# ScalarE writes the high parts of keys and queries straight from PSUM, and VectorE's subtraction frees the bank

## What is computed

```python
x = x + xattn(layernorm(x), ctx, ctx, mask, W_q, W_k, W_v, W_o)   # x 32x100x128, ctx 32x1444x128
x = x + ffn(layernorm(x), gate_w, w1, w2)                          # 8 experts, best 2 per token

# xattn: 16 heads of 8
q = split(Q @ W_q.T); k = split(K @ W_k.T); v = split(V @ W_v.T)
scores = clip(einsum('bhqd,bhkd->bhqk', q, k) / sqrt(8), -50, 50)
attn = exp(scores) / sum(exp(scores))
out = einsum('bhqk,bhkd->bhqd', attn, v) @ W_o.T
```

## Time and profile before

| | |
|---|---|
| median of 3 runs | 1106.81 us (1106.25 to 1107.64) |
| the profiled execution's own time | 1106.66 us |
| its span, first to last instruction | 1104.9 us |
| granted TensorE clock, mean of the span | 0.969 |
| TensorE busy | 94% |
| ScalarE busy | 70% |
| VectorE busy | 69% |
| GpSimd busy | 22% |

### The profile page before, as it was taken

How to read it: one execution, slowest core, us unless ns; L and a number is a source line. 1 busy time by engine, 2 the same in 40 slices (tenths; PEclk the granted TensorE clock), 3 DMA queues, 4 the chain that set the end, 5 groups by cost and what they waited for, 6 DMA issues and landing times.

```text
span 1104.9 us, 32396 instructions
## 1 busy us (share of the span) xinstructions
PE 1033.4 (94%) x10544; PEld 759.8 (69%) x10545; DVE 761.0 (69%) x2088; ACT 769.6 (70%) x1088; POOL 240.0 (22%) x320
## 2 busy tenths in 40 slices
PE   5789999999999999999999999999999999399990
PEld 3567677777777677777677777777767776299990
DVE  4567777777777777777777777777777777444433
ACT  2567877777777877777877777877778777144430
POOL 3331111111111111111111111111111111245554
PEclk8899999999999999999999999999999999699995
DMA  7645555455555554555455555555555544022216
GB/s 217 186 154 166 173 170 170 165 166 167 168 171 170 172 171 164 173 167 170 167 171 173 173 173 173 174 174 174 174 174 174 174 157 142 23 68 63 65 49 178
DMA packets 144319, 172.71 MB, mean 156 GB/s; under 512 B 32235, under 2 KB 88559, under 8 KB 144287
## 3 DMA queue, kind: packets, MB, share of 16 engines
q1 hardware_dynamic: 138622, 165.26, 45.4%
q0 software_dynamic: 4896, 6.63, 2.2%
q10 hardware_dynamic: 768, 0.41, 0.2%
HBM read 36.83 MB, written 22.08 MB: 53 GB/s over the span
## 4 chain that ended last, share of the span: by engine, by line
PE 90%; DMA 3%; POOL 2%; SPq 2%; DVE 1%; issue 1%; ACT 1%; ACTq 0%; POOLq 0%; DVEq 0%
PE scores L753 31%; PE o_sum L765 26%; PE scratch L687 7%; PE scratch L676 7%; PE scores L873 5%; PE scores L884 5%; PE scratch L671 4%; PE scratch L726 1%; SPq L535 1%; POOL w_sb L597 1%; PE scratch L681 1%; PE scratch L731 1%; DMA x_all<-in_x_dram 1%; DMA q_stack<-q_rep 1%; PE scratch L747 1%
## 5 line engine op out<-in xcount | busy, mean ns | idle before, releaser
L990 ACT ACTIVATE probs<-scores 128x800 f32<-128x800 f32 (+1 forms) x640 | 615.2, 975 | 160.7 <-PE scores L753 158.6
L753 PE MATMUL scores<-q_stack,k_stack 128*128 128x400 f32 x1536 | 415.2, 380 | 10.5 <-DMA q_stack<-q_rep 8.1
L1136 DVE TENSOR_SCALAR probs<-probs 128x800 f32<-128x800 f32 (+1 forms) x640 | 396.2, 654 | 25.2 <-ACT probs L990 25.0
L753 PEld LDWEIGHTS scores<-q_stack,k_stack 128*128 128x128 f32 x1536 | 249.2, 190 | 110.5 <-issue 100.9
L765 PE MATMUL o_sum<-probs,v_both 128*17 128x200 f32 x6144 | 316.3, 335 | 0.1
L765 PEld LDWEIGHTS o_sum<-probs,v_both 128*17 128x17 f32 x6144 | 151.1, 97 | 132.4 <-issue 71.9
L630 POOL DMA_INDIRECT expert_rows<-rows,row_atu x64 | 75.6, 1181 | 408.8 <-DVE row_atu L1233 361.4
L687 PE MATMUL scratch<-w_turned,ctxT 128*128 128x128 f32 x768 | 102.5, 277 | 0.0
L687 PEld LDWEIGHTS scratch<-w_turned,ctxT 128*128 128x128 f32 x768 | 101.2, 194 | 0.0
L1073 DVE COPY v_both<-scratch 128x512 f32<-128x512 f32 x93 | 64.4, 692 | 42.4 <-PE scratch L687 42.4
L1048 DVE CAST k_hi<-k_full 128x512 fp32r<-128x512 f32 (+1 forms) x93 | 38.4, 412 | 79.5 <-ACT k_full L932 79.4
(11 more groups left out here) (145 smaller groups left out, 771.1 us busy)
## 6 DMA issues: line engine op xcount, KB each, us to landing
k_stack<-k_hi SPq DMA_DIRECT2D x192, 256.0 KB, 2.5
k_stack<-k_lo SPq DMA_DIRECT2D x192, 256.0 KB, 2.6
expert_rows<-fill SPq DMA_DIRECT2D x32, 406.2 KB
xT_and_ctx<-in_ctx_dram SPq DMA_DIRECT2D x16, 704.0 KB
ctx_nat<-in_ctx_dram SPq DMA_DIRECT2D x16, 704.0 KB
q_rep<-q_parts SPq DMA_DIRECT2D x124, 50.0 KB, 1.9
q_stack<-q_rep SPq DMA_DIRECT2D x124, 50.0 KB, 1.9
v_both<-expert_rows SPq DMA_DIRECT2D x57, 65.0 KB, 1.8
```

Source lines behind the costliest of these rows:

```text
L753: last = nc.tensor.matmul(score_banks(c)[:, m, :], k_stack[p][:, g, t * P:(t + 1) * P], q_stack[p][:, :, g, :], start=True, stop=True)
L990: nc.scalar.activation(probs_of(c), score_banks(c), ACT.Exp, scale=SCALE).then_inc(exp_ready, 1)
L1136: nc.vector.tensor_scalar(chunk, chunk, LOW, HIGH, ALU.max, ALU.min).then_inc(probs_ready, 1)
```

## The change

ScalarE's copy of a key or query step now goes straight into the high part, `k_hi` or `q_parts[:, 0]`, and takes over the wait for the DMAs that read that tile before. VectorE waits for ScalarE's copy and subtracts the high part from the bank in PSUM; this subtraction now frees the bank. The copies `k_full` and `q_full`, VectorE's casts of them, and the semaphore `q_split` are gone; SP, and ScalarE for the first queries, wait for the bank to be freed instead (`k_split` stays for the first batch). The expert stage, which used a part of `k_full`, has a tile of its own (`hidden_sb`). Order and chunks of the steps stay.

```diff
--- before.py
+++ after.py
@@ -198,8 +198,7 @@
                    sb("ctx_nat1", [P, TILES, D])[:]]
         w1_sb = xT_and_ctx[:, 0:E * F].rearrange("p (e f) -> p e f", e=E)
         ctxT = sb("ctxT", [P, TILES * P])
-        k_full = sb("k_full", [P, KSTEPS, KC * P])
-        q_full = sb("q_full", [P, SQ])
+        hidden_sb = sb("hidden_sb", [P, 2, FC * P])
         k_hi = sb("k_hi", [P, TILES * P], F32R)
         k_lo = sb("k_lo", [P, TILES * P], F32R)
         k_stack = [sb(f"k_stack{p}", [P, GROUPS, TILES * P], F32R) for p in range(2)]
@@ -271,7 +270,7 @@
         tile_home = [sb(f"tile_home{n}", [P, 1], U32) for n in range(NB)]
         w1_tile = ctxT[:, 0:2 * F].rearrange("p (n f) -> p n f", n=2)
         tileT = ctxT[:, 2 * F:2 * F + 2 * P].rearrange("p (n r) -> p n r", n=2)
-        hiddenT = k_full[:, 0:2, :].rearrange("p n (c r) -> p n c r", c=FC)
+        hiddenT = hidden_sb[:].rearrange("p n (c r) -> p n c r", c=FC)
 
         y_all = [probs[0:SQ].rearrange("p u q -> p (u q)")[:, 0:B * D].rearrange("q (b d) -> q b d", b=B),
                  xT_and_ctx[0:SQ, 0:E * F].rearrange("q (b d) -> q b d", b=B)]
@@ -318,7 +317,6 @@
         scratch_emptied = [sem(f"scratch_emptied{n}") for n in range(2)]
         k_hi_ready = sem("k_hi_ready")
         k_split = sem("k_split")
-        q_split = sem("q_split")
         k_stacked = [sem(f"k_stacked{k}") for k in range(KSTEPS)]
         scores_ready = sem("scores_ready")
         exp_ready = sem("exp_ready")
@@ -395,6 +393,16 @@
             first = FIRST_UNIT[c] % RING_UNITS
             return probs[:, first:first + UNITS[c], :]
 
+        def keys_split_at(b, k):
+
+            return scratch_use(b - 1, STEPS.index(("key", k)))
+
+        def queries_split_at(n):
+
+            if isinstance(n, int) and n < 2:
+                return divmod(ALONE.index(("first query", n)), 2)[::-1]
+            return scratch_use(n - 2, STEPS.index(("query", 0)))
+
         def all_emptied(engine, b, n):
 
             for late in range(2):
@@ -450,7 +458,12 @@
             def stack_keys(p, b):
 
                 for k in range(KSTEPS):
-                    sp.wait_ge(k_split, KSTEPS * b + k + 1)
+                    if later(b):
+                        bank, use = keys_split_at(b, k)
+                        sp.wait_ge(scratch_emptied[bank], use + 1)
+                        carry_wait(sp, sp_passed)
+                    else:
+                        sp.wait_ge(k_split, k + 1)
                     cols = slice(k * KC * P, (k + 1) * KC * P)
                     for t, part in enumerate((k_hi, k_lo, k_hi, k_lo)):
                         sp.dma_start(k_stack[p][t:P:4, :, cols].bitcast(F32),
@@ -458,7 +471,8 @@
 
             def spread_queries(n):
 
-                sp.wait_ge(q_split, n + 1)
+                bank, use = queries_split_at(n)
+                sp.wait_ge(scratch_emptied[bank], use + 1)
                 carry_wait(sp, sp_passed)
                 if later(n):
                     sp.wait_ge(q_stacked, QD * n)
@@ -927,16 +941,15 @@
                 elif name == "turn":
                     nc.scalar.copy(ctxT[:, KEY_COLS[k]], scratch[:, bank, 0:KEYS[k]]).then_inc(scratch_emptied[bank], 1)
                 elif name == "key":
-                    if later(b):
-                        act.wait_ge(k_split, KSTEPS * (b - 1) + k + 1)
-                    nc.scalar.copy(k_full[:, k, 0:KEYS[k]], scratch[:, bank, 0:KEYS[k]]).then_inc(scratch_emptied[bank], 1)
+                    act.wait_ge(k_stacked[k], KD * b)
+                    nc.scalar.copy(k_hi[:, KEY_COLS[k]], scratch[:, bank, 0:KEYS[k]]).then_inc(k_hi_ready, 1)
                 elif name == "first query":
                     if k:
-                        act.wait_ge(q_split, k)
-                    nc.scalar.copy(q_full[:], scratch[:, bank, 0:SQ]).then_inc(scratch_emptied[bank], 1)
+                        act.wait_ge(q_spread, QS * k)
+                    nc.scalar.copy(q_parts[:, 0, :], scratch[:, bank, 0:SQ]).then_inc(q_hi_ready, 1)
                 elif name == "query":
-                    act.wait_ge(q_split, b + 1)
-                    nc.scalar.copy(q_full[:], scratch[:, bank, 0:SQ]).then_inc(scratch_emptied[bank], 1)
+                    act.wait_ge(q_spread, QS * (b + 1))
+                    nc.scalar.copy(q_parts[:, 0, :], scratch[:, bank, 0:SQ]).then_inc(q_hi_ready, 1)
                 elif name == "queries":
                     nc.scalar.copy(attnT[:], scratch[:, bank, 0:SQ]).then_inc(scratch_emptied[bank], 1)
                 else:
@@ -954,7 +967,8 @@
 
             def spread_first():
 
-                act.wait_ge(q_split, 1)
+                bank, use = queries_split_at(0)
+                act.wait_ge(scratch_emptied[bank], use + 1)
                 for t in range(4):
                     act.dma_start(q_rep[t:P:4, :, :].bitcast(F32), q_parts[:, t // 2, :].bitcast(F32)).then_inc(q_spread, 16)
 
@@ -1042,24 +1056,16 @@
 
                 cols = KEY_COLS[k]
                 bank, use = at
-                dve.wait_ge(scratch_emptied[bank], use + 1)
-                if later(b):
-                    dve.wait_ge(k_stacked[k], KD * b)
-                nc.vector.tensor_copy(k_hi[:, cols], k_full[:, k, 0:KEYS[k]]).then_inc(k_hi_ready, 1)
                 dve.wait_ge(k_hi_ready, KSTEPS * b + k + 1)
-                nc.vector.tensor_tensor(k_lo[:, cols], k_full[:, k, 0:KEYS[k]], k_hi[:, cols].bitcast(F32),
-                                        ALU.subtract).then_inc(k_split, 1)
-
-            def split_queries(b, at):
+                nc.vector.tensor_tensor(k_lo[:, cols], scratch[:, bank, 0:KEYS[k]], k_hi[:, cols].bitcast(F32),
+                                        ALU.subtract).then_inc(scratch_emptied[bank], 1)
+
+            def split_queries(n, at):
 
                 bank, use = at
-                dve.wait_ge(scratch_emptied[bank], use + 1)
-                if later(b):
-                    dve.wait_ge(q_spread, QS * b)
-                nc.vector.tensor_copy(q_parts[:, 0, :], q_full[:]).then_inc(q_hi_ready, 1)
-                dve.wait_ge(q_hi_ready, b + 1)
-                nc.vector.tensor_tensor(q_parts[:, 1, :], q_full[:], q_parts[:, 0, :].bitcast(F32), ALU.subtract
-                                        ).then_inc(q_split, 1)
+                dve.wait_ge(q_hi_ready, n + 1)
+                nc.vector.tensor_tensor(q_parts[:, 1, :], scratch[:, bank, 0:SQ], q_parts[:, 0, :].bitcast(F32),
+                                        ALU.subtract).then_inc(scratch_emptied[bank], 1)
 
             def split(name, k, b, at):
```

## The result

The changed kernel takes 1121.86 us (median of 4 runs, 1120.6 to 1122.3) beside 1106.53 us of the kernel before on the same chip: ratio 1.0135, 95% interval 1.0118 to 1.0153. It is slower by 15.3 us; the forecast was 21.2 us slower, and 1121.9 lies 0.6 us under its range. The profiled execution took 1121.89 us, its span is 1120.0 us.

A forecast was written before the change was run, and what follows sets the result against it. TensorE was taken to pace the loop: 30 batches times a 0.72 us pause is 21.6, minus 0.4 for the first batch, plus 21.2 us on 1106.66, giving 1127.9 us; range 1122.5 to 1136.

The forecast's parts named there:

- The one cost: Query after key 1: the bank is freed later, by VectorE's subtraction, so TensorE stands 0.72 us in each batch.
- Rival 1: Loop: the ring of score banks, not TensorE, sets the pace and absorbs the pause; 1106.3 us; chance 0.06.
- Rival 2: Loop: each of 30 pauses lowers TensorE's clock, costing 1.7 us as after an earlier pause; 1179 us; chance 0.02.
- Casts in the loop: Loop: VectorE's key casts, 38.4 us in all, lie beside TensorE's work, so removing them is worth 0.
- The subtraction: VectorE's subtraction reading PSUM stays at 0.69 us for a full step, despite the skill's larger fixed cost.
- ScalarE's rounding copy: ScalarE's key copy into the rounded tile stays at 0.56 us mean; upper case 0.10 us more for a full step.
- The moved waits of ScalarE and SP: ScalarE's copies wait for earlier DMAs, SP for the subtraction under another semaphore; ScalarE's key-copy wait was judged free.
- the bound of 0.24: Very start: the first query's cast leaves, ScalarE's second query copy waits; between minus and plus 0.24 us, taken as 0.
- Nothing is spare: Query after key 1: its load came as the scores ran out, so the later bank costs 0.72 us, start against start.
- minus 0.4: First batch: a 2 us query pause is absorbed by TensorE's later GpSimd wait; GpSimd's chain starts 0.4 us earlier.

The follow-up runs named there:

- the doubled run: Changed kernel with VectorE subtracting key 1 twice, first into a spare tile, the second freeing the bank: 1138.28 us, ratio 1.0289.
- the move by a chunk: Kernel before with only the query taken one chunk later: 1104.37 us, ratio 0.9978; a second time 1104.54 us, ratio 0.9982.
- the queries by the old way: Changed kernel with q_full, VectorE's cast of the queries and q_split back, keys as changed: 1120.71 us, ratio 1.013.
- the casts from PSUM: Changed kernel, query a chunk later, plus in the first batch only a VectorE cast from PSUM ahead of each key's subtraction: ratio 0.9948.
- the run with the longer target: Changed kernel with one more, long-met wait and its worked-out number in front of ScalarE's key copy: 1122.13 us, ratio 1.0133.
- the two with extra subtractions: Changed kernel, query a chunk later, first batch only: one more VectorE subtraction per key, inputs in SBUF (ratio 0.9950) or from PSUM (0.9940).
- the keys alone: Kernel before, query a chunk later, with the change of the keys in the first batch only: ratio 0.9957.

## Why the forecast was right in kind and 6 us too high

**Right.** The one cost is the wait of the query for key 1's bank, in its place, with its releaser and its size: 0.71 to 0.73 us against the kernels without it (28.852 against 28.138 and 28.121), forecast 0.72, and it is added in full. Rival 1 is refuted: with the pause gone the batch falls by just the pause, and one twice as long costs 0.60 us more. Rival 2 as well: 27 pauses of 0.5 us, and of 1.1 us in the doubled run, leave the granted clock at 1.00 over 786 us. The Trainium skill ("TensorE: Matmul & The Clock Gate", section on psum-queue depth-cycling) tells of a kernel whose short idle spells between groups made the clock swing; the one spell per batch here did not. Casts in the loop are worth nothing (90 put back, the batch 28.128 us). The subtraction takes no longer out of PSUM: 657 against 662 ns. The larger fixed cost with a PSUM source that the Trainium skill ("VectorE: DVE Perf Modes", section on the TRN2 errata) gives is not seen in these two means. ScalarE's rounding copy takes what its plain one took, 563 ns. The moved waits of ScalarE and SP cost at most 0.02 us a batch (28.138 with the query later, against 28.116 in the kernel before with the same move), and the start moved by 0.16 us, inside the bound of 0.24.

**Wrong, three terms** (6.2 us, of which the start gave back 0.16).
1. *"Nothing is spare"*: 29 batches came out at 0.66 us each, not 0.72, which is 1.7 us. The sum took the query's start of the earlier trace rows as the end of TensorE's own work. It was already 0.07 us late, for ScalarE's copy, which stood behind its wait and the arithmetic for that wait's target; the change takes this away. The sign was in the row: the load there has idle time in front of it and comes 0.14 us after the copy's end, the very delay that I had taken from the earlier trace rows for a signal. That load was waiting, as the move by a chunk showed.
2. *"minus 0.4" for the first batch*, the step that failed most: 3.3 us. The sum let the pause at the query be absorbed by a wait for GpSimd's rows that would stay, because GpSimd's chain would move forward by the one cast ahead of it and keep its length. It did not keep it. Its first two norm groups, before:

```profile
45.77 5.02 POOL L597 TENSOR_SCALAR w_sb<-x_all,moments,rstd 100x128 f32<-100x128 f32 x4
...
54.12 5.27 POOL L597 TENSOR_SCALAR w_sb<-x_all,moments,rstd 100x128 f32<-100x128 f32 x4
```

and after:

```profile
45.34 4.41 POOL L611 TENSOR_SCALAR w_sb<-x_all,moments,rstd 100x128 f32<-100x128 f32 x4
...
52.44 4.17 POOL L611 TENSOR_SCALAR w_sb<-x_all,moments,rstd 100x128 f32<-100x128 f32 x4
```

The second ended 22.7 instead of 25.6 us after the first scores. So the rows were there before TensorE asked: its 3.8 us of waits went, and the pause of 1.7 us was paid in full. With the waits went the fall of the clock that the earlier trace rows already showed: 0.28 of 6 us, 1.7 us. I had counted that row as the price of a pause, in rival 2, and not as something that goes with the wait it follows. Minus 2.1, minus 1.7 and plus 0.66 for batch 1's pause make minus 3.1; measured minus 2.95. That this closes to 0.15 us is in part luck, for two smaller terms are left out: TensorE's waits for exponentials rose from 0.5 to 1.3 us, and the clock, still low after the start, came up sooner (granted 0.50 and 0.92 in the two stretches of 3 us from 36 us before, 0.55 and 1.00 after, some 0.4 us). What shortened GpSimd's groups is in part open.
3. *The end of the run*: minus 1.2 us, for which the sum had no term. No step of the change touches this stretch but the tile of the hidden rows, which was tried and cleared. The clock explains 0.2 of it; the rest is open.

A rule that would have pointed at the second term stands in the Trainium skill ("SBUF — State Buffer", section on SBUF's two separate sides): a VectorE instruction in a two-port mode, or with two inputs in SBUF beside a GpSimd instruction that reads SBUF, and a GpSimd instruction shut each other out of a shared port pair, whichever starts first. The rows agree for the casts from SBUF (a norm of 1.30 us beside one, 0.83 beside a cast from PSUM). For subtractions with two inputs in SBUF they are mixed: a norm took 1.14 us beside 0.45 us of one, and others 0.79 beside 0.45 and 0.87 beside 0.65. The clips would fit the rule if they run in such a mode, which no row here shows.

## What to carry to other kernels

When a slower engine takes over the freeing of a buffer, find the one consumer that comes next behind it, take start against start, and multiply; here that gave the cost of a batch to 0.06 us (0.72 against 0.66), and moving that consumer by one place took it back whole: the changed kernel with the query a chunk later is faster than both (ratios 0.9937 and 0.9923 to the kernel before). Price the edges of the run apart from the loop: work off an idle engine was worth nothing in the loop, where TensorE is full, and some 3 us in the first batch, where TensorE waited, because a wait, what slows the engine waited for, and a slower clock behind the wait can go together. And a consumer that starts one signal's delay after its releaser may already be waiting, though no wait row says so, as the query was by 0.07 us.

## What the runs showed of the hardware

- One more wait that had long been met, with the arithmetic for its target (instructions of 35 ns on ScalarE's queue), delayed the copy behind it, and TensorE with it, by 0.07 us: 28.852 and 28.919 us a batch without and with it.
- Pauses of nearly one length had different ends for the clock. After 1.6 to 1.7 us at the first batch's query the granted clock stayed 1.00 in the changed kernel, with the queries by the old way and with the casts from PSUM; it fell in the run with the longer target (0.61 from 47 to 50 us) and in the two with extra subtractions (0.51 and 0.62 from 48 to 51). After 2.3 us there it stayed 1.00 in the doubled run; 2.2 us for the norms were followed by 0.50 with the keys alone. A wait of 2.8 to 3.4 us for the norms was followed by 0.50 to 0.52 (60 to 63 us) in all four profiles that had one.
- VectorE's rounding cast of 128x512 took 0.43 us from SBUF and 0.69 us from PSUM, while its subtraction took 0.69 us from either.
- A norm on GpSimd (100x128, float32) took 0.79 to 0.93 us beside no clip and no cast of VectorE from SBUF, and 1.01 to 2.09 us beside 0.4 us or more of clips, in 18 traces.
